# Identity times identity on TensorE inside the normalization helper of a four-layer decoder kernel

## The chip, the cores and the metric

The kernel runs on one NeuronCore of one Trainium2 chip. The metric is the device time of one execution in microseconds, given as the median of several runs. Beside these runs stands one execution that the hardware profiler recorded. All rows below come from that one.

## The reference, cut to what matters

The model takes 4 sequences of 512 tokens, 128 wide, and a context of 77 tokens for each sequence. It adds twelve sublayers to the residual x, three in each of four layers: a self attention, an attention over the context, and a feed-forward sublayer (mixtures of experts, or, in the third layer, an attention with mixed experts and a dense network behind it). Each sublayer reads a normalized x:

```
def _layernorm(x, axis=-1, eps=1e-05):
    m = jnp.mean(x, axis=axis, keepdims=True)
    v = jnp.var(x, axis=axis, keepdims=True)
    return (x - m) / jnp.sqrt(v + eps)
...
x = x + _L1_attn_ref(_layernorm(x, axis=-1), L1_attn_wq, L1_attn_wk, L1_attn_wv, L1_attn_wo, L1_attn_bo)
x = x + _L1_xattn_ref(_layernorm(x, axis=-1), ctx_1024, L1_xattn_w_sim, L1_xattn_b_sim, L1_xattn_W_qv, L1_xattn_b_qv)
x = x + _L1_ffn_ref(_layernorm(x, axis=-1), ...)
```

With the normalization inside the third layer's feed-forward sublayer that is followed by a projection, the kernel's helper is called 13 times. All matrix products are of float32 or of its split halves.

## The kernel before

The tokens lie on 128 partitions in 16 tiles of 128 tokens by 128 features: four batches of four tiles. The residual `T.X`, the normalized tokens `T.LNX` and their transpose `T.LNT` stay in SBUF for the whole kernel. Sublayers run one after another. Each is first a call of `layernorm` (L100), a block of its own, and then one block or more of work. At a block's end every engine waits for all others.

Inside the block of `layernorm`, SyncE issues the next stage's loads. VectorE computes the statistics that the sublayer before has not left (most have left all), adds epsilon to the variances (L132), ScalarE takes the root (L168), and VectorE makes the reciprocal and the shift (L136, L137). Then both scale tiles of 128x128: VectorE the even ones (L142), ScalarE the odd ones (L171). TensorE waits for the four tiles of a batch and transposes them into PSUM bank c (L162; banks 2 and 3 are called `twin`). ScalarE copies banks 0 and 2 to `T.LNT` (L176), VectorE banks 1 and 3 (L149), each after its last scaled tile. Batch 3's copy on VectorE is the last thing of the block, or nearly.

`T.ident` is the identity of 128x128 in float32, loaded once before the first stage. PSUM bank 7 isn't used by `layernorm`.

One call, that of the third layer's context attention (stage `l2x`, L1919), passes `aside`: work of that stage that needs no normalized tokens. Its part on TensorE is three products of 308 columns (L1899, L1900), issued ahead of the transposes. On VectorE two multiplications that read them (L1906) and four additions (L1911) stand between the scaled tiles and the copies.

What follows a normalization, where it matters below: `l1a` (L1461, L1463), `l1m` (the router, L1079, 32 products of 64 columns, then the shared expert, L1028 and L1029), `l0m` (the same with 16 columns), `l2a` (L1737), and `l2f` (L3029).

Of the kernel before, what the change touches and what calls it, by code (L numbers as in the profile page):

```python
# [21 lines left out]
P = 128  # L22
# [27 lines left out]
def chain(T, dve):  # L50

    def link(ins):
        T.dve_steps += 1
        ins.then_inc(T.dve_step, 1)
        dve.wait_ge(T.dve_step, T.dve_steps)
    return link


def token_stats(nc, T, link, src, tiles):

    for t in tiles:
        out = nc.vector.bn_stats(T.ln_stats[:, t, :], src[:, t, :])
    link(out)
    for t in tiles:
        out = nc.vector.bn_aggr(T.ln_mv[:, t, :], T.ln_stats[:, t, :])
    T.ln_known += tiles
    return out
# [32 lines left out]
def layernorm(nc, T, src, dst, dstT, loads=(), load_sem=None, more=(), more_sem=None, begun=(), times=None, aside=None, columns=None, eps=1e-5, zeros=()):  # L100

    n = T.ln_calls
    T.ln_calls += 1
    with nc.Block() as block:
        @block.sync
        def _(sp):
            for to, frm in loads:
                sp.dma_start(to, frm).then_inc(load_sem, 16)  # L110
            for to, frm in more:
                sp.dma_start(to, frm).then_inc(more_sem, 16)
            for to, frm, here in begun:
                sp.dma_start(to, frm).then_inc(here, 16)

        @block.gpsimd
        def _(pool):
            for sems, _ in T.used:
                for s in sems:
                    pool.sem_clear(s)  # L120
            for buffer in zeros:
                nc.gpsimd.memset(buffer, 0.0)

        @block.vector
        def _(dve):
            link = chain(T, dve)
            unknown = [t for t in range(NT) if t not in T.ln_known]
            if unknown:
                link(token_stats(nc, T, link, src, unknown))
            T.ln_known = []  # L130
            if times is None:
                nc.vector.tensor_scalar(T.ln_var_eps[:, :], T.ln_mv[:, :, 1], eps, None, ALU.add).then_inc(T.ln_var, 1)  # L132
            else:
                nc.vector.tensor_scalar(T.ln_var_eps[:, :], T.ln_mv[:, :, 1], times, eps, ALU.mult, ALU.add).then_inc(T.ln_var, 1)
            dve.wait_ge(T.ln_std, n + 1)
            link(nc.vector.reciprocal(T.ln_rstd[:, :], T.ln_var_eps[:, :]))  # L136
            nc.vector.scalar_tensor_tensor(T.ln_shift[:, :], T.ln_mv[:, :, 0], -1.0, T.ln_rstd[:, :], ALU.mult, ALU.mult)\  # L137
                .then_inc(T.ln_scaled, 1)
            dve.wait_ge(T.ln_scaled, n + 1)
            for t in range(NT):  # L140
                if t % 2 == 0:
                    nc.vector.tensor_scalar(dst[:, t, :], src[:, t, :], T.ln_rstd[:, t:t + 1], T.ln_shift[:, t:t + 1],  # L142
                                            ALU.mult, ALU.add).then_inc(T.ln_even, 1)
            if aside is not None:
                aside[1](dve)
            for c in range(1, B, 2):
                dve.wait_ge(T.ln_turned, B * n + c + 1)
                if columns is None:
                    nc.vector.tensor_copy(dstT[:, c * S:(c + 1) * S], T.bank[c][:, :])  # L149
                else:  # L150
                    nc.vector.tensor_scalar(dstT[:, c * S:(c + 1) * S], T.bank[c][:, :], columns[:, 0:1], columns[:, 1:2],
                                            ALU.mult, ALU.add)

        @block.tensor
        def _(pe):
            if aside is not None:
                aside[0](pe)
            for c in range(B):
                pe.wait_ge(T.ln_even, NT // 2 * n + TPB // 2 * (c + 1))
                pe.wait_ge(T.ln_odd, NT // 2 * n + TPB // 2 * (c + 1))  # L160
                for t in range(TPB):
                    last = nc.tensor.transpose(T.bank[c][:, t * P:(t + 1) * P], dst[:, c * TPB + t, :], T.ident[:, :])  # L162
                last.then_inc(T.ln_turned, 1)

        @block.scalar
        def _(act):
            act.wait_ge(T.ln_var, n + 1)
            nc.scalar.activation(T.ln_var_eps[:, :], T.ln_var_eps[:, :], ACT.Sqrt).then_inc(T.ln_std, 1)  # L168
            act.wait_ge(T.ln_scaled, n + 1)
            for t in range(1, NT, 2):  # L170
                nc.scalar.activation(dst[:, t, :], src[:, t, :], ACT.Identity, bias=T.ln_shift[:, t:t + 1],  # L171
                                     scale=T.ln_rstd[:, t:t + 1]).then_inc(T.ln_odd, 1)
            for c in range(0, B, 2):
                act.wait_ge(T.ln_turned, B * n + c + 1)
                if columns is None:
                    nc.scalar.activation(dstT[:, c * S:(c + 1) * S], T.bank[c][:, :], ACT.Copy)  # L176
                else:
                    nc.scalar.activation(dstT[:, c * S:(c + 1) * S], T.bank[c][:, :], ACT.Identity, bias=columns[:, 1:2],
                                         scale=columns[:, 0:1])
            if aside is not None:  # L180
                aside[2](act)
    for _, held in T.used:
        held.close()
    T.used = []
# [3160 lines left out]
```

## Time and profile before

| | |
|---|---|
| median of three runs | 2374.95 us |
| the three runs | 2374.86, 2374.95, 2377.97 us |
| the profiled execution | 2371.28 us |
| its span | 2369.5 us |
| TensorE busy in it | 2107.8 us, 89% |
| VectorE busy | 1673.9 us, 71% |
| ScalarE busy | 1216.1 us, 51% |
| GpSimd busy | 1148.7 us, 48% |
| granted TensorE clock, mean | 0.94 of full |

A busy TensorE isn't TensorE at its peak: matmuls are pipelined, and a row's duration holds the latency too, so that what a product costs in a stream is the distance between starts. The granted clock is the share of full speed that the chip gave TensorE: 1.00 stands for 2.4 GHz, 0.50 for 1.2 GHz. In the first 31.9 us the profile has no record of it and shows 1.00 throughout.

### The profile page before, as it was taken

What the parts mean: (1) busy time and instruction counts of PE and PEld (TensorE: products, weight loads), DVE (VectorE), ACT (ScalarE), POOL (GpSimd) and SP (SyncE); (2) the same over time, 40 slices, a digit from 0 to 9 for tenths busy, and PEclk for the clock granted to TensorE, in tenths of its full rate; (3) what the DMA queues carried; (4) which work ended last, traced back from release to release, by engine and by line L of the source; (5) the groups of instructions that cost most, each with busy time, mean ns of one, the idle gap of its engine ahead of it and who ended that gap; (6) DMA issues with size and microseconds to landing.
All of it is one profiled execution on the core that took longest, in us unless ns stands there. A gap on an engine that the chain in (4) does not pass through costs nothing. (4 is left out here: it accounts for less than half of the span.)

```text
span 2369.5 us, 37661 instructions
## 1 busy us (share of the span) xinstructions
PE 2107.8 (89%) x12788; PEld 1466.2 (62%) x12788; DVE 1673.9 (71%) x3561; ACT 1216.1 (51%) x2586; POOL 1148.7 (48%) x1343
## 2 busy tenths in 40 slices
PE   6999789667899997759999999999999986979889
PEld 3666557556588875545666666666666644647666
DVE  5778777654788884667777777777766665379578
ACT  6888645322466654535445454444444443444455
POOL 5332027101499981137676766667665623004255
PEclk8999979866999998979999999999999997989899
DMA  1000006000566630022343333343443341000085
GB/s 50 2 2 2 7 21 155 8 6 22 125 153 157 155 83 24 1 70 59 96 101 76 99 84 95 79 108 79 92 92 78 73 89 43 8 1 1 14 201 125
DMA packets 65048, 161.92 MB, mean 68 GB/s; under 512 B 8139, under 2 KB 19147, under 8 KB 57560
## 3 DMA queue, kind: packets, MB, share of 16 engines
q1 hardware_dynamic: 64856, 159.50, 28.9%
q8 instruction: 103, 1.69, 0.3%
q14 instruction: 89, 0.73, 0.1%
HBM read 156.46 MB, written 3.01 MB: 67 GB/s over the span
## 5 line engine op out<-in xcount | busy, mean ns | idle before, releaser
L2636 PE MATMUL bank<-l2h_og,l2h_wo 128*128 128x512 f32 x512 | 260.4, 593 | 1.6 <-DVE LNT L2897 1.6
L2746 ACT ACTIVATE l2h_pr<-twin,l2h_nmx 128x512 f32<-128x512 f32 x256 | 176.0, 688 | 150.5 <-PE bank L2625 104.9
L2738 ACT ACTIVATE l2h_prT<-bank 128x512 f32<-128x512 f32 x256 | 151.9, 593 | 194.6 <-PE bank L2625 194.6
L1215 POOL TENSOR_TENSOR l1m_hid_lo<-l1m_hid,l1m_hid_hi 128x512 fp32r<-128x512 f32 x128 | 210.3, 1663 | 46.0 <-ACT l1m_hid_hi L1142 45.6
L2900 DVE TENSOR_REDUCE l2h_nmx<-twin 128x2 f32<-128x1024 f32 x128 | 156.1, 1220 | 90.7 <-PE twin L2614 90.6
L2975 POOL TENSOR_TENSOR l2h_vs<-l2h_vg 128x256 f32<-128x256 f32 x256 | 192.9, 754 | 19.9 <-DVE l2h_vg L2873 19.9
L2873 DVE TENSOR_TENSOR l2h_vg<-bank,l2h_gv 128x512 f32<-128x512 f32 x256 | 174.9, 683 | 34.2 <-POOL l2h_vs L2975 20.9
L2885 DVE TENSOR_TENSOR l2h_og<-bank,l2h_gt 128x512 f32<-128x512 f32 x256 | 173.1, 680 | 3.8 <-PE bank L2636 2.7
L2970 POOL TENSOR_TENSOR l2h_plain<-l2h_plain,l2h_rotated 128x512 f32<-128x512 f32 x64 | 82.6, 1291 | 169.5 <-DVE l2h_rotated L2866 169.5
L2625 PE MATMUL bank<-ident,l2h_pr 128*128 128x128 f32 x1024 | 160.8, 279 | 0.0
L2625 PEld LDWEIGHTS bank<-ident,l2h_pr 128*128 128x128 f32 x1024 | 116.7, 140 | 66.9 <-issue 43.4
L2599 PE MATMUL bank<-l2h_w_hi,l2h_x_hi 128*128 128x512 f32 x256 | 150.8, 589 | 4.1 <-DVE l2h_vg L2873 3.9
L405 ACT ACTIVATE l0a_pr<-l0a_sc,l0a_nmx 128x128 f32<-128x128 f32 (+3 forms) x256 | 133.3, 553 | 22.2 <-DVE l0a_nmx L290 21.4
L1265 DVE TENSOR_TENSOR l1m_hid<-l1m_prod,l1m_c 128x512 f32<-128x512 f32 x128 | 135.6, 1059 | 4.4
L2978 POOL TENSOR_TENSOR l2h_vs<-l2h_vs 128x128 f32<-128x128 f32 x256 | 121.5, 475 | 20.1
L2650 PE MATMUL bank<-l2h_prT,l2h_v 128*64 128x256 f32 x1024 | 124.7, 385 | 0.0
L1257 DVE TENSOR_TENSOR l1m_prod<-bank,l1m_gate 128x512 f32<-128x512 f32 x128 | 88.1, 688 | 45.7 <-ACT l1m_gate L1177 33.8
L1177 ACT ACTIVATE l1m_gate<-bank 128x512 f32<-128x512 f32 x128 | 76.6, 599 | 84.6 <-PE bank L1020 84.6
L2356 POOL TENSOR_TENSOR l3x_pr<-l3x_pr,l3x_rs 128x1232 f32<-128x1232 f32 x16 | 35.9, 2249 | 171.6 <-DVE l3x_rs L2378 171.6
L2983 POOL TENSOR_TENSOR l2h_v<-l2h_vs 128x64 f32<-128x64 f32 x256 | 82.2, 321 | 74.9 <-PE bank L2650 57.2
L2650 PEld LDWEIGHTS bank<-l2h_prT,l2h_v 128*64 128x64 f32 x1024 | 68.2, 136 | 75.2 <-issue 41.7
L2636 PEld LDWEIGHTS bank<-l2h_og,l2h_wo 128*128 128x128 f32 x512 | 95.5, 189 | 28.5 <-issue 3.8
(625 smaller groups left out, 5823.3 us busy)
## 6 DMA issues: line engine op xcount, KB each, us to landing
l2h_gt<-l2m_gate_rows SPq DMA_DIRECT2D x128, 512.0 KB, 7.3
l1m_c<-l1m_weights SPq DMA_DIRECT2D x62, 512.0 KB, 6.5
l3m_c<-l3m_weights SPq DMA_DIRECT2D x30, 512.0 KB, 6.6
l0m_c<-l0m_weights SPq DMA_DIRECT2D x14, 512.0 KB, 6.8
l1m_w<-in_l1m_pairs SPq DMA_DIRECT2D x32, 192.0 KB, 6.5
l2h_fresh<-in_l2m_wqkv SPq DMA_DIRECT2D x8, 768.0 KB, 4.2
l2h_wo<-in_l2m_wo SPq DMA_DIRECT2D x8, 512.0 KB, 3.9
l0m_w<-in_l0m_pairs SPq DMA_DIRECT2D x8, 192.0 KB, 5.3
```

The source lines that it names most:

```text
L1215: nc.gpsimd.tensor_tensor(hid_lo[:, h % RING, :], hid[:, h % HELD, :], hid_hi[:, h % RING, :], ALU.subtract)\
L1265: nc.vector.tensor_tensor(hid[:, h % HELD, :], p, cslot[s][:, blk * S:(blk + 1) * S], ALU.mult).then_inc(hidden, 1)
L2599: out = nc.tensor.matmul(pj[at % 2][:, :], x[:, b * S + t * P:b * S + (t + 1) * P], w[:, QK + h * S:QK + (h + 1) * S], start=(p == 0), sto ...
L2625: out = nc.tensor.transpose(tbank[:, c * P:(c + 1) * P], pr[:, h, c * P:(c + 1) * P], T.ident[:, :])
L2636: nc.tensor.matmul(ybank[:, :], wo[s][:, e, :], og[:, e % 4, :], start=(e == 0), stop=(e == E - 1))\
L2650: out = nc.tensor.matmul(obank[g % 2][h * HD:(h + 1) * HD, half * 2 * P:(half + 1) * 2 * P], v[:, g % 2, h * TPB + c, :], prT[:, half, h, ...
L2738: nc.scalar.activation(prT[:, j // 2 % 2, h, :, j % 2 * P:(j % 2 + 1) * P], tbank[:, :].rearrange("p (c q) -> p c q", c=TPB), ACT.Copy).th ...
L2746: nc.scalar.activation(pr[:, h, :], sbank[:, h, :], ACT.Exp, bias=nmx[:, k % 2, h:h + 1], accum_out=rs[:, g % 2, t, h:h + 1]).then_inc(exp ...
L2873: nc.vector.tensor_tensor(vg[:, u % 2, :, :], pj[at % 2][:, :].rearrange("p (e d) -> p e d", e=E), spread(gv_h[s][:, b * TPB + t, h, :], H ...
L2885: nc.vector.tensor_tensor(og[:, e % 4, :], obank[g % 2][:, :], gt[:, e // 4, e % 4, :], ALU.mult)\
L2900: nc.vector.tensor_reduce(nmx[:, k % 2, :], sbank[:, :, :], axis=AX, op=ALU.max, negate=True)\
L2975: nc.gpsimd.tensor_tensor(vs[:, u % 2, :, :], vg[:, u % 2, 0:4, :], vg[:, u % 2, 4:8, :], ALU.add)\
```

## The change

Two groups of matrix products are added to TensorE's part of `layernorm`. Each multiplies the identity by itself and writes 128 columns of bank 7, which nothing reads there. Nine stand at the block's start, ahead of `aside`'s products, and two ahead of each batch but the first, before the wait for its scaled tiles. Nothing is removed or moved. In 13 calls that makes 195 products.

```
         @block.tensor
         def _(pe):
+            def keep_busy(times):
+
+                for _ in range(times):
+                    nc.tensor.matmul(T.bank[7][:, 0:P], T.ident[:, :], T.ident[:, :], start=True, stop=True)
+            keep_busy(9)
             if aside is not None:
                 aside[0](pe)
             for c in range(B):
+                if c:
+                    keep_busy(2)
                 pe.wait_ge(T.ln_even, NT // 2 * n + TPB // 2 * (c + 1))
                 pe.wait_ge(T.ln_odd, NT // 2 * n + TPB // 2 * (c + 1))
                 for t in range(TPB):
```

## Rows read from the trace of the kernel before

**Rows 1.** The page: busy time (share of the span), and granted clock in 40 slices.
```profile
PE 2107.8 (89%) x12788; PEld 1466.2 (62%) x12788; DVE 1673.9 (71%) x3561; ACT 1216.1 (51%) x2586; POOL 1148.7 (48%) x1343
...
PEclk8999979866999998979999999999999997989899
```

**Rows 2.** Timeline of the fourth normalization, ahead of stage l1a: start, duration, instructions, idle before.
```profile
434.81 0.17 DVE L132 TENSOR_SCALAR ln_var_eps<-ln_mv 128x16 f32<-128x16 f32 x1 [0.30 <-PEq L969]
...
435.76 3.19 ACT L171 ACTIVATE LNX<-X,ln_shift,ln_rstd 128x128 f32<-128x128 f32 x8 [0.53 <-DVE ln_shift L137]
...
436.78 1.94 PE L162 MATMUL bank<-ident,LNX 128*128 128x128 f32 x8 [6.44 <-ACT LNX L171]
438.52 1.92 PE L162 MATMUL twin<-ident,LNX 128*128 128x128 f32 x8
...
440.47 0.69 DVE L149 COPY LNT<-twin 128x512 f32<-128x512 f32 x1 [1.01 <-PE twin L162]
...
441.46 2.04 PE L1461 MATMUL bank<-LNT,l1a_wq 128*128 128x512 f32 x2 [1.03 <-PEq L106]
```

**Rows 3.** Line 162 in all 13 normalizations: durations min/median/max in ns.
```profile
L162 PE MATMUL bank<-ident,LNX x104: 272/421/448, 14.1 to 2222.0; 128*128 128x128 f32 x104
```

**Rows 4.** Timeline, streams of 128-column products at each level of the clock.
```profile
563.77 0.64 PE L1632 MATMUL bank<-l1c_w,l1c_hq 128*128 128x128 f32 x2
...
564.20 0.63 PE L1633 MATMUL bank<-l1c_w,l1c_ehq 128*128 128x128 f32 x2
...
946.62 3.65 PEld L1771 LDWEIGHTS bank<-l2a_v,l2a_e 128*128 128x128 f32 x32 [1.78 <-DVE l2a_v L1829]
```

**Rows 5.** Windows: length, busy (count) by engine, PEclk, DMA share, GB/s; runs of TensorE at 1.2 GHz.
```profile
441.40:444.90 3.50, 3.44 (x6) 2.15 (x7) 0.92 (x1) 0.00 (x0) 0.00 (x0) 0.50 0.01 2
444.90:446.00 1.10, 1.10 (x5) 0.59 (x4) 0.00 (x0) 0.00 (x0) 0.00 (x0) 0.99 0.00 0
500.00:502.90 2.90, 2.88 (x14) 2.84 (x15) 1.83 (x6) 2.72 (x8) 0.00 (x0) 0.50 0.22 74
502.90:503.50 0.60, 0.48 (x4) 0.24 (x2) 0.09 (x1) 0.55 (x1) 0.00 (x0) 0.96 0.00 0
...
561.00:567.70 6.70, 6.25 (x29) 6.16 (x30) 0.36 (x1) 1.35 (x2) 0.00 (x0) 0.50 0.00 0
567.90:568.50 0.60, 0.41 (x4) 0.22 (x2) 0.15 (x1) 0.00 (x0) 0.00 (x0) 1.00 0.00 0
```

**Rows 6.** Timeline of the eighth normalization, the one with `aside`.
```profile
952.81 1.72 PE L1899 MATMUL bank<-l2p_ctxT,l2p_wk 128*128 128x308 f32 x4 [2.35 <-PEq L1729]
...
955.83 0.86 DVE L1906 TENSOR_TENSOR l2p_krot<-bank,l2p_ktrig_kept 128x308 f32<-128x308 f32 x2
...
959.27 0.68 DVE L149 COPY LNT<-twin 128x512 f32<-128x512 f32 x1
```

**Rows 7.** Windows behind normalizations 6 (l1m), 7 (l2a) and 10 (l2f).
```profile
577.30:588.20 10.90, 10.88 (x37) 8.66 (x38) 2.52 (x4) 6.51 (x10) 5.96 (x5) 0.50 0.01 2
...
897.70:902.20 4.50, 4.42 (x9) 2.38 (x10) 0.85 (x2) 0.00 (x0) 1.66 (x3) 0.50 0.09 33
1960.30:1963.80 3.50, 3.48 (x4) 1.50 (x5) 1.40 (x1) 0.69 (x1) 3.20 (x3) 0.50 0.01 2
```

**Rows 8.** Timeline, the first transposes of normalizations 3 and 12, with the idle time before.
```profile
324.54 1.94 PE L162 MATMUL bank<-ident,LNX 128*128 128x128 f32 x8 [3.49 <-ACT LNX L171]
...
2116.71 1.86 PE L162 MATMUL bank<-ident,LNX 128*128 128x128 f32 x8 [4.63 <-ACT LNX L171]
```

**Rows 9.** Windows: the 16-column router behind normalization 3, what follows it, and normalization 12.
```profile
329.20:332.20 3.00, 2.98 (x27) 3.00 (x28) 0.00 (x0) 2.98 (x6) 2.30 (x2) 1.00 0.00 0
332.40:339.00 6.60, 6.60 (x12) 3.35 (x13) 4.68 (x15) 2.96 (x4) 3.60 (x4) 0.50 0.00 1
...
2116.70:2117.40 0.70, 0.63 (x4) 0.39 (x4) 0.70 (x4) 0.70 (x3) 0.00 (x0) 1.00 0.00 0
2117.50:2120.80 3.30, 2.77 (x12) 2.31 (x12) 1.51 (x4) 2.45 (x6) 0.00 (x0) 0.50 0.00 0
```

More of the change, by code:

```diff
@@ L155, in _, with keep_busy @@
         def _(pe):
+            def keep_busy(times):
+                for _ in range(times):
+                    nc.tensor.matmul(T.bank[7][:, 0:P], T.ident[:, :], T.ident[:, :], start=True, stop=True)
+            keep_busy(9)
             if aside is not None:
@@ L158, in _ @@
             for c in range(B):
+                if c:
+                    keep_busy(2)
                 pe.wait_ge(T.ln_even, NT // 2 * n + TPB // 2 * (c + 1))
```

## Prediction

> **What bounds the kernel now.** I read the page first. TensorE is busy for 89% of the span, but its clock isn't at full speed everywhere: the row of slices has sixes, sevens and eights, and several lie where normalizations are [rows 1]. So two questions follow: what bounds a normalization, and at which clock TensorE runs in it and right behind it.
>
> The timeline of one normalization answers the first [rows 2]. From VectorE's first instruction (434.81) a chain of small ones leads to the scaled tiles (435.76), and TensorE's first transpose starts at 436.78, 1.97 us after entry. TensorE is idle through all of these 1.97 us, and for some time before them too: 6.44 us in all here, 3.49 to 4.63 in seven others [rows 2, 8]. Then 16 transposes run until VectorE's copy of the last bank begins at 440.47, and TensorE's next stage starts at 441.46 after 1.03 idle. ScalarE scales its last tile until 438.95, so the last batch would be ready about 1.5 us before that copy: it is TensorE that ends the block, because it is slow. The two groups of eight transposes start 1.74 apart, 0.217 each. The source view says that this is the usual case: the median transpose lasts 421 ns, the fastest 272 [rows 3].
>
> The second I read from windows around each call. Of 13 normalizations none ran at 2.4 GHz throughout, seven ran at 1.2 GHz from the first transpose to the last, three (5, 11 and 13) rose in the last few transposes, 8 halfway, and 9 and 12 began high and fell after a batch. Behind four of them (4, 6, 7, 10) the next stage starts low and TensorE's busy time fills the stretch: 3.5, 11.0, 4.5 and 3.5 us [rows 5, 7].
>
> **The price of one added product.** The trace has no product of the identity with itself, but it has streams of the same shape. At 1.2 GHz pairs of 128-column products start 0.43 apart, 0.215 each; at 2.4 GHz 32 weight loads of the same shape take 3.65, 0.114 each, with the matmuls hidden behind them [rows 4]. The bounds are therefore 0.107 (half of the low price) and 0.215.
>
> **The nine at the start.** At the low clock 9 x 0.215 = 1.94 us against 1.97 of waiting: they just fit. At the high clock they take about 1 us and leave 1 us of idleness. The cover is the chain of variance, root, reciprocal, shift and two tiles on each of the other engines. It is gone if the first product starts late: the first pair of a low stream above takes 0.59 instead of 0.43, so up to 0.15 can stick out. I take 0.1 in each of 12 calls: **+1.2 us**, between 0 and 1.8. The first call has much more cover, since it computes its statistics inside the block.
>
> **The six between the batches.** At the low clock they are not covered. A batch costs 4 x 0.217 = 0.87, while ScalarE gives the next one every 0.80 (3.19 for eight tiles). The queue is TensorE's own, so all six are added: 6 x 0.215 = 1.29 us at the block's end, if the clock stays low. The transposes behind them are late, then the copies of banks 2 and 3, then the block's end. At the high clock a batch with its two takes 0.65 and fits into 0.80, the last batch ends 0.43 after ScalarE's last tile, and the last copy begins at about 439.6 instead of 440.47: 0.85 earlier.
>
> So all hangs on where the clock rises. What the added products change is that TensorE works without a break from entry, 1.94 us earlier, until the end: up to 6.7 us instead of 3.6. The trace shows when unbroken runs at the low clock brought a rise: after 2.9 us (500.02 to 502.9, fourteen transposes, with 4.3 idle ahead), after 3.5 us (441.4 to 444.9), and only after 6.1 where the run began at 561.7 [rows 5]; no unbroken run of wide products lasted longer without one. I take the rise as equally likely anywhere from 2.7 to 6.1 us after entry, 0.7 to 4.1 after the first transpose. If it comes x after the first transpose, of 3.45 + 1.29 = 4.74 of low-clock work the rest is halved: the end is at 2.37 + x/2, not before 2.87 (ScalarE). The mean is 3.6, against 3.45 where it was low throughout and a mean of 3.35 over the twelve. That is +0.25 each, 12 x 0.25 = **+3.0 us**, with bounds of -0.85 and +1.3 each.
>
> Here a rule of the Trainium skill speaks against the change, so it is weighed. In the window from 500.0 to 502.9 TensorE did only float32 transposes, and at its end the clock was up, for two further normalizations as well [rows 5]. The page "TensorE: Matmul & The Clock Gate", section "Part 4: PE-mode transpose", says that transposes don't count as busy for the clock. By that rule the sixteen transposes would help nothing, the added products alone would seldom bring a rise, and the sum of this paragraph and the last would be about +17 us instead of +4; the trace disagrees with it.
>
> **The eighth normalization.** There nine products stand ahead of three of the stage's own that are already on the path: VectorE goes straight from its scaled tiles to L1906 at 955.83, with no idle time before it, and L1906 reads two of them; four additions and the copies behind it, to 959.95, end the block [rows 6]. Nothing covers the nine. They cost 0.97 to 1.94, by the clock, and I take the middle: **+1.5 us**.
>
> **What follows.** Behind 4, 7 and 10 the next stage's first 3.5, 4.5 and 3.5 us ran at 1.2 GHz with TensorE busy all the time [rows 5, 7]. At 2.4 GHz they take half: -1.75, -2.25 and -1.75. The idle gap between the block and the next is 1.03 us [rows 2], and ahead of normalization 12 the high clock outlived 4.63 us of idleness by a batch [rows 8, 9]. So if it rose in the normalization I expect it to last in 85 of 100: **-4.9 us**. Behind 6 stand 32 router products of 64 columns and the shared expert's, 11.0 us at the low clock, TensorE the one everybody waits for [rows 7]. Halved that is -5.5. But narrow products don't hold the clock well: behind 3 the 16-column router began at the high clock and lost it at 332.3 without a pause [rows 9]. With 64 columns I give it 60 of 100: **-3.3 us**. The same stretch behind 3 was lucky, since the clock was up for nearly all of its router (27 of 32 in 3.0 us, 0.11 each [rows 9]). On average it will have half of that: **+1.4 us**. Behind 2, 5 and 9 TensorE idles again before it has much work, so nothing is carried over; behind 11 and 12 the clock was high already.
>
> **Sum.** 1.2 + 3.0 + 1.5 - 4.9 - 3.3 + 1.4 = -1.1 us. On the profiled execution's 2371.28 that is 2370.2; on the median of the runs, 3.7 us above it, 2373.8. The unchanged kernel's own runs lie 3.1 us apart, and I put that down, as a guess, to the clock rising and falling at other places in each. What a measurement can tell from no change is about 0.2%, 4.7 us.
>
> **The rivals.**
>
> *The clock stays up.* TensorE idles only 1.5 to 2.7 us before entry in most calls, once the 1.97 behind it are filled. If the clock never falls there, or rises as early as it can, each of twelve normalizations gives about 0.6 (of at most 0.85), the stages behind give 11.3, and with 8 and the start's cost the sum is -7.2 - 11.3 + 1.0 + 0.5 = -17: 2358. For it: normalization 12 had the high clock for its first batch after 4.6 us of idling and lost it only 0.7 us later [rows 8, 9]. Against it: in 4, 7, 10 and 11 TensorE idles 4.5 us and more before entry even so, and at the high clock the nine leave 1 us idle again. Half of this effect, -8, is more likely than all of it: 2367.
>
> *The rise is given back.* The clock rises in the normalizations, but the block's gap or the next stage's narrow products lose it, and nothing is gained behind: 1.2 + 3.0 + 1.5 + 1.4 = +7: 2382. It decides the sign as soon as less than about 7 us comes from behind.
>
> *The clock doesn't rise in time.* If it falls within the nine, they are done early at the high clock, an idle piece follows, and the next rise comes only after the block. Then the six cost their full 1.29: 12 x 1.29 + 1.8 + 1.9 = +19: 2394, and if this holds for half of the calls, 2383. The deciding point is a rise later than about 2.2 us after the first transpose. For it: seven normalizations now have no rise in 3.6 us of dense work. Against it: the work is now nearly twice as long.
>
> *Nothing happens*, because every added product is hidden. At the low clock the six can't be, so this I count with the forecast.
>
> **How the numbers follow.** The forecast, gains and costs within 4.7 us of each other, gets 0.48; the clock that stays up, in part or in full, 0.30; the rise given back 0.12; the rise too late 0.10. Of the second a little ends inside the bound and of the forecast a little outside, which evens out: faster 0.30, same 0.48, slower 0.22. The likeliest case alone spans 2370 to 2379. The range must reach into both neighbours: 2363 (a bit more than half of the first rival) to 2382 (the second).
>
> **What would show it.** In the profile after, L162 should follow the nine without a gap at the low clock, its first start 1.97 to 2.1 after L132. Windows should show the clock at 1.00 before the last batch in most normalizations, and VectorE's last copy 5.1 to 7.0 after L132 (5.66 now). Line 1461, L1737 and L3029 should start at 1.00. L1906 should start 1 to 2 us later after L134 than now. The prediction is wrong if windows stay at 0.50 through the block, if the last copies move beyond 6.5 as a rule, or if the stages behind start low as before.

## The result and the profile after

The change made the kernel slower: 0.7% where it was first timed, 1.0068 times the kernel before (95% interval 1.0048 to 1.0088; median 2396.11 us against 2375.65, six runs each), and 1.0037 (1.0018 to 1.0055) in a second set (median 2386.09 us of nine against 2380.01). Its times lie in two groups, to which the fourth experiment returns, and the median goes with how many fall in each. The forecast was no change, 2373.8 us within 2363 to 2382. The profiled execution took 2398.32 us with a span of 2396.5, 27.0 more than the span before. Its line for the added products on the page, in the columns of part 5 (busy, mean ns of one, idle before):

```profile
L159 PE MATMUL bank<-ident 128*128 128x128 f32 x390 | 72.5, 347 | 54.1 <-PEq L3086 16.6
```

The source adds 195 products and the trace counts 390. Lines below L153 have moved by seven, so that L162, L171 and L176 are now L169, L178 and L183. The timeline of normalization 4, to set beside [rows 2]:

```profile
442.60 4.18 PE L159 MATMUL bank<-ident 128*128 128x128 f32 x18 [4.46 <-PEq L976]
...
443.56 3.19 ACT L178 ACTIVATE LNX<-X,ln_shift,ln_rstd 128x128 f32<-128x128 f32 x8 [0.53 <-DVE ln_shift L137]
...
446.57 1.06 PE L169 MATMUL bank<-ident,LNX 128*128 128x128 f32 x4
447.43 0.85 PE L159 MATMUL bank<-ident 128*128 128x128 f32 x4
...
448.99 0.60 PE L169 MATMUL twin<-ident,LNX 128*128 128x128 f32 x4
449.43 0.61 PE L159 MATMUL bank<-ident 128*128 128x128 f32 x4
...
449.88 0.60 PE L169 MATMUL twin<-ident,LNX 128*128 128x128 f32 x4
450.51 0.69 DVE L149 COPY LNT<-twin 128x512 f32<-128x512 f32 x1 [1.08 <-PE twin L169]
```

Read it against [rows 2] step by step. Nine products are eighteen records and fill TensorE for 3.97 us, from 442.60 to 446.57, where the tiles were ready at 1.97. Two products are four records. At the high clock a group of four transposes starts 0.45 after the four records ahead of it, and the next pair of products 0.44 after the transposes: a batch now takes 0.89, where ScalarE gives one every 0.80 and where, with the tiles all ready, transposes alone would take 0.44. L132 starts at 442.61, so that the last copy starts 7.90 after it; before, it was 5.66.

The windows (columns as in [rows 5]) show that the clock did what the added work was to bring, in the normalizations and right behind them:

```profile
446.50:451.10 4.60, 3.98 (x30) 3.74 (x28) 1.28 (x2) 1.45 (x3) 0.00 (x0) 0.85 0.02 4
451.50:454.00 2.50, 2.49 (x10) 1.79 (x10) 0.92 (x1) 0.00 (x0) 0.00 (x0) 1.00 0.01 3
...
904.40:908.70 4.30, 4.24 (x20) 4.27 (x21) 2.74 (x11) 3.41 (x9) 1.15 (x1) 0.50 0.58 150
908.80:911.50 2.70, 2.70 (x27) 2.70 (x26) 0.69 (x1) 1.12 (x2) 0.00 (x0) 1.00 0.82 246
912.80:917.00 4.20, 2.97 (x13) 1.85 (x14) 0.90 (x3) 1.24 (x4) 1.63 (x3) 1.00 0.00 0
```

The stretch behind normalization 4, low for 3.5 us in [rows 5], is now at 1.00, and so is the one behind 7, low for 4.5 in [rows 7].

To see where 27.0 us went I cut both traces at each start of L132 (L134 in normalization 8) and at the end of the last copy to `T.LNT`. The first piece is the normalization from there on, the second what lies between it and the next one's L132.

| piece | before, us | after, us | difference |
|---|---|---|---|
| 13 normalizations, sum | 82.3 | 101.5 | +19.2 |
| normalization 4 | 6.35 | 8.59 | +2.2 |
| normalization 8 | 7.14 | 9.27 | +2.1 |
| normalization 9 (after: clock high throughout, as in 13) | 6.27 | 6.06 | -0.2 |
| behind 4, 7 and 10 | 56.88, 55.33, 46.93 | 55.08, 53.15, 45.18 | -5.7 |
| behind 6 | 314.12 | 316.30 | +2.2 |
| behind 9 | 931.46 | 938.04 | +6.6 |
| behind 13, to the end | 145.0 | 147.7 | +2.7 |
| behind 1, 2, 3, 5, 8, 11 and 12 | | | +2.1 |

The normalizations are the greater part. Of the rest, the stage behind 9 is the largest. A window of each trace, from the same stage:

```profile
1062.80:1093.10 30.30, 24.74 (x139) 15.84 (x139) 17.73 (x24) 15.88 (x33) 23.09 (x40) 1.00 0.38 78
```

```profile
1076.00:1093.10 17.10, 13.95 (x42) 7.95 (x41) 5.76 (x8) 5.08 (x9) 9.97 (x21) 0.60 0.11 26
```

The first is of the kernel before, the second of the one after, where the stage begins 13 us later; both start 40.7 to 40.9 us into it. Before, the clock was up for good by then; after, it was down for most of the stretch (0.60 granted). No instruction there differs.

### The profile page after: what moved, and what is told of

The parts are those of the page before. It is cut to its first block and busy times, and to the rows that moved or that the text cites. A ratio compares the mean times of both kernels' runs of the same rounds, so it can differ in the third digit from the quotient of the medians.

```text
span 2396.5 us, 38441 instructions
## 1 busy us (share of the span) xinstructions
PE 2154.4 (90%) x13178; PEld 1515.9 (63%) x13178; DVE 1678.4 (70%) x3561; ACT 1217.2 (51%) x2586; POOL 1149.5 (48%) x1343
## 3 DMA queue, kind: packets, MB, share of 16 engines
q8 instruction: 106, 1.74, 0.3%
## 5 line engine op out<-in xcount | busy, mean ns | idle before, releaser
L159 PE MATMUL bank<-ident 128*128 128x128 f32 x390 | 72.5, 347 | 54.1 <-PEq L3086 16.6
L1184 ACT ACTIVATE l1m_gate<-bank 128x512 f32<-128x512 f32 x128 | 76.6, 599 | 84.8 <-PE bank L1027 84.8
```

## The experiments

All edits are to the changed kernel. From the fifth experiment on the pairs between the batches are out, even where the lines shown don't say it; only the eighth has one product there. Ratios are to the kernel before, timed on the same chip in the same rounds.

**The same products as transposes.** Each float32 product becomes one transpose, which is one record.

```
-                    nc.tensor.matmul(T.bank[7][:, 0:P], T.ident[:, :], T.ident[:, :], start=True, stop=True)
+                    nc.tensor.transpose(T.bank[7][:, 0:P], T.ident[:, :], T.ident[:, :])
```

> All 195 added products become transposes of the identity into the same bank (one pass over 128 columns each, where a float32 product is two: the profile after counts 18 matmul records for nine). Theory A, the price of a product was off by two and the rest of the working stands: added work halves, 9 x 0.215 = 1.94 us fits into the 1.97 us of waiting, so the first transpose of the real work is at 1.97 to 2.1 us after L132, the sum over the 13 normalizations (82.3 us before, 101.5 after) comes to 82 to 87, and the median is 2370 to 2378. Theory B, the price of a product is not the matter and any added work on TensorE in this place costs (a disturbance of the stages behind, a later clock): 2385 or more, and the stages behind normalization 9 stay 6 us longer than before. Theory C, transposes don't lift the clock: normalizations near 88 us in sum and the stages behind 4, 7 and 10 as long as before, 2378 to 2384.

Measured: 0.9992 (0.9979 to 1.0004), median 2377.59 us, no difference. The normalizations last 84.8 us in sum, and the first real transpose comes 1.97 us after L132 in twelve of the thirteen. This is theory A's outcome, and B falls by the time. One sign that B named did appear: the stage behind 9 took 940.35 us, 8.9 more than before. So that stage grows without the price of a product, and its 6.6 us in the table aren't part of that price. C falls too: the normalizations are not near 88, and behind 4, 7 and 10 the stages take 55.1, 51.45 and 45.2 us. What I had forecast for the change is what this kernel does.

**Only the nine at the start.**

```
-                if c:
-                    keep_busy(2)
```

> Only the nine products at the start. Theory A: TensorE reaches the first real transpose 3.4 to 4.0 us after L132 where the clock is low at entry, as with the change, so some 15 of the 19 us that the normalizations became longer stay, the six between batches give back 0.3 to 0.5 each: normalizations 94 to 97 us in sum, the median 2384 to 2392. Theory D, the six between the batches are what costs: the sum near 86 and the median under 2380.

Measured: 0.9966 (0.9954 to 0.9978), median 2373.86 against 2380.01 for the kernel before: faster. The normalizations last 83.2 us, not the 94 to 97 that I expected: theory A was wrong about where in the change the cost sits, and D was right. The timeline of its normalization 4 shows why:

```profile
434.46 3.61 PE L159 MATMUL bank<-ident 128*128 128x128 f32 x18 [4.46 <-PEq L974]
434.46 0.17 DVE L132 TENSOR_SCALAR ln_var_eps<-ln_mv 128x16 f32<-128x16 f32 x1 [0.30 <-PEq L974]
437.90 1.04 PE L167 MATMUL bank<-ident,LNX 128*128 128x128 f32 x8
438.77 1.04 PE L167 MATMUL twin<-ident,LNX 128*128 128x128 f32 x8
...
439.85 0.69 DVE L149 COPY LNT<-twin 128x512 f32<-128x512 f32 x1 [0.18 <-PE twin L167]
```

The nine do delay the first transpose, to 3.44 us after L132. But by then nearly all scaled tiles lie ready, and the clock has risen, so eight transposes take 0.87 instead of 1.74 [rows 2]. The last copy starts 5.39 after L132, sooner than the 5.66 of before. The clock in the second group of transposes and just ahead of it:

```profile
438.00:439.80 1.80, 1.80 (x17) 1.57 (x15) 0.69 (x1) 1.52 (x4) 0.00 (x0) 1.00 0.01 2
```

**Only the two between batches.** `keep_busy(9)` is taken out.

> Only the two products ahead of batches 1 to 3. Theory A: the first real transpose is at 1.97 us as before; six products are 2.6 us at the low clock and 1.3 at the high one, part of it in ScalarE's shadow: normalizations +0.7 to +1.3 each, 91 to 98 in sum, less 3 us behind normalizations that now end at the high clock; median 2379 to 2388. Theory D: as slow as the whole change, 2390 or more.

Measured: 1.0055 (1.0043 to 1.0067), median 2393.4: D's case, as slow as the whole change. The normalizations last 106.8 us, above A's 91 to 98 and 5.3 more than with the whole change: put in ahead of these pairs, the nine gave time back. In number 4, TensorE reaches its first transposes at 1.97 us as before and then alternates:

```profile
442.63 1.08 PE L168 MATMUL bank<-ident,LNX 128*128 128x128 f32 x4 [6.44 <-ACT LNX L177]
443.51 1.06 PE L159 MATMUL bank<-ident 128*128 128x128 f32 x4
444.37 1.06 PE L168 MATMUL bank<-ident,LNX 128*128 128x128 f32 x4
```

A pair of products costs 0.86 us at the low clock, as much as the four transposes that wait behind it; three pairs are 2.6 us.

**The change once more.**

> The change as it is, once more, on the same chip. Its six times so far fall in two groups, 2383 to 2386 and 2396 to 2398. Theory A says only that the mean is about 2394 and that the gap between the groups lies in which stages run at 1.2 GHz, so a profile of another execution differs in the stages behind the normalizations, not in the normalizations by more than 3 us. Theory B: the slow group is a fixed cost, the times gather at 2396 and 10 us of it sit in the same stage, the one behind normalization 9.

Measured: 1.0037 (1.0018 to 1.0055), times from 2382.5 to 2398.8 with a gap between 2386.1 and 2392.6. The profile is again of the slower group: 101.1 us of normalizations and 938.04 behind 9. So it doesn't tell the groups apart. Two further profiles were taken for that.

> The change unchanged, for a profile of its faster group (2382 to 2386), which about half of its 15 times so far belong to; both profiles so far are of the slower one (2396.5 and 2397.0 us of span). If this one is of the faster group: by the clock's theory the 13 normalizations last 98 to 102 us as in the others and the 10 to 14 us lie in several stages, the one behind normalization 9 (938.0 us in both) at 931 to 935 among them. By the rival, that the added products themselves are costlier in the slower group, the normalizations last 90 us or less.

> The same once more, with the same expectations, since a single profile falls into the faster group only about every second time.

Both fell in the slower group as well (2398.29 and 2399.84 us). Their normalizations last 102.7 and 101.9 us. In the first the stage behind 9 took 933.94, four less than in the others, and the whole was no faster. None of the four profiles is of the faster group, so no trace shows in which stages the two part. The granted clock of the 17 executions does tell them apart: its mean over the span is 0.947 to 0.951 in the seven up to 2386.5 us, and 0.942 to 0.946 in the ten from 2392.6. The means of the groups, 0.9491 and 0.9438, are apart by some 25 us more at the low clock; if TensorE sets the pace in them, half of that is lost, 12 to 13 us (an estimate), and the groups' mean times lie 12.3 apart. That the clock makes the gap is thus likely; what decides between the two cases stays open.

**The nine, but not in normalization 8.**

```
-            keep_busy(9)
+            if aside is None:
+                keep_busy(9)
```

> The nine products at the start alone, and none in normalization 8, where three products of the stage wait behind them. With the nine, normalization 8 lasted 8.71 us against 7.14 before. Theory E, the nine are paid back everywhere but there: normalization 8 back at 7.1, the rest as with the nine alone, 1 to 2 us faster than those, 0.995 to 0.997 of the kernel before. Rival F, the nine gain by the clock in the stage behind normalization 8 too: 54.3 us there becomes 55.9 again and the time is that of the nine alone.

Measured: 0.9978 (0.9964 to 0.9992), no faster than with it (0.9966). Normalization 8 is back at 7.13, but the stage behind it at 55.88: rival F's numbers. The nine cost 1.58 us there, and the clock that they lift gives 1.57 back in the projection behind.

**Nine transposes at the start, nothing between.** The edits of the first two experiments together.

> Nine transposes of the identity at the start, one pass each, and nothing between the batches. Theory G, what pays is the time TensorE works without a break ahead of the real transposes: 1.94 us instead of 3.9, so the clock rises in fewer normalizations before their transposes; the first real transpose is at 1.97, normalizations 5.6 to 6.4 each, 77 to 80 in sum (83.2 with nine products), the stages behind 4, 7 and 10 partly at the low clock; 2372 to 2377 where the kernel before is at 2380. Rival H, added transposes don't count for the clock: normalizations as before, 82 in sum, and the time of the kernel before.

Measured: 0.9963 (0.9950 to 0.9976), median 2369.68 against 2377.48; normalizations 76.8 us in sum, behind 4, 7 and 10 54.4, 51.46 and 45.18. Theory G holds for the normalizations, but not in that the rise comes in fewer of them: in ten they take 5.64 to 5.92 us, against 5.95 to 6.47 before. The first and the last take 6.36 and 6.25, the eighth 7.13.

```profile
435.90 2.15 PE L159 MATMUL bank<-ident 128*128 128x128 f32 x9 [4.47 <-PEq L974]
...
437.88 1.48 PE L167 MATMUL bank<-ident,LNX 128*128 128x128 f32 x8
439.42 1.40 PE L167 MATMUL twin<-ident,LNX 128*128 128x128 f32 x8
```

```profile
435.90:437.80 1.90, 1.90 (x9) 1.75 (x9) 1.55 (x7) 1.16 (x4) 0.00 (x0) 0.50 0.30 83
437.90:440.70 2.80, 2.60 (x17) 2.00 (x16) 1.79 (x6) 2.80 (x8) 0.00 (x0) 0.85 0.28 79
```

Nine records fit into the 1.97 us, the clock rises among the real transposes, and ScalarE's last tile ends the block. TensorE did nothing but transposes here, and rival H falls. The Trainium skill's page "TensorE: Matmul & The Clock Gate", section "Part 4: PE-mode transpose", has it that transposes don't count as busy; for these float32 ones the trace disagrees.

**Six products behind the last batch, with the nine.**

```
                 last.then_inc(T.ln_turned, 1)
+            keep_busy(6)
```

> Nine products at the start, and six more behind the last batch's transposes, where they run beside the copies and nobody waits. Theory I, the six cost only because they stand ahead of batches: the normalizations stay at the 83 us of the nine alone, the time within 3 us of the nine alone, or below it where the clock now outlives the gap to the next block (behind 6 above all, 317 us there with the nine alone against 314). Rival J, added work on TensorE is what costs wherever it stands: near the change's own 2386 to 2396. At 1.2 GHz six products are 2.6 us against some 1.8 us until the next block, so up to 0.8 can stick out in a normalization where the clock hasn't risen.

Measured: 1.0019 (1.0008 to 1.0030), median 2383.72 against 2377.48. Theory I fell: behind the last batch the six cost too. Rival J, that they cost wherever they stand, comes nearer, though the time is below J's 2386 to 2396. The trace shows a place that neither named, the block's end:

```profile
442.69 1.50 PE L159 MATMUL bank<-ident 128*128 128x128 f32 x12
444.49 1.10 PE L1467 MATMUL bank<-LNT,l1a_wq 128*128 128x512 f32 x2 [0.30 <-PEq L106]
```

The next block waits for TensorE, which is done at 444.19, while VectorE's copy ended at 443.58. The next stage starts 0.91 after that copy's end; with the nine alone it starts 0.30 after it (440.54, 440.84). That is 0.6 in this call. Over the thirteen, this gap sums to 16.4 us, with the nine alone to 10.1: 6.3 more, beside +3.2 in the normalizations (86.4). The two make up 9.5 of the 14.8 us by which this profile's span exceeds that of the nine alone; the rest lies in the stages behind.

**One product between the batches.** `keep_busy(1)` for `keep_busy(2)`.

> The change with one product between the batches instead of two. Theory A' (each product ahead of a batch is two passes, 0.215 us at the high clock and 0.43 at the low one, and none of it is hidden once the nine have let the tiles be ready): half of the step from the nine alone (83 us in the normalizations, 0.9966) to the change (101 us, 1.0037 to 1.0068): normalizations 90 to 94, the time 0.999 to 1.002 of the kernel before. Rival K, one product of 0.215 at the high clock fits behind a batch of 0.43 into ScalarE's 0.80 a batch: normalizations as with the nine alone.

Measured: 1.0015 (1.0000 to 1.0030); normalizations 90.7 us. Both lie where A' put them, and K falls: the sums run 83.2, 90.7, 101.5 for none, one and two.

**Eighteen transposes for nine products.** The edits of the sixth experiment, with `keep_busy(18)`.

> Eighteen transposes at the start, nothing between the batches: as many passes over 128 columns as nine products. Theory A'' (only passes count, for time and clock alike): the profile looks like that of the nine products alone, first real transpose 3.3 to 4.0 us after L132 in most normalizations, normalizations 82 to 84 in sum, the time 0.995 to 0.998 of the kernel before. Rival L, a product costs or lifts the clock otherwise than two transposes: outside these.

Measured: 0.9975 (0.9963 to 0.9987), normalizations 85.9 us, first real transpose 3.2 to 3.9 us after L132 in most. The time is that of nine products within the intervals. The sum is 1.9 us above the 82 to 84 that I had set as the border to rival L, so by its letter L isn't ruled out. A product counts as two transposes to within that: the sums are 83.2 and 85.9, and what the 2.7 between them are due to wasn't tried.

**Nine transposes, and four behind the last batch.**

> Nine transposes at the start as in the kernel of that name (76.8 us of normalizations, 0.9963), and four more transposes behind the last batch. They take 0.43 us at the high clock and 0.86 at the low one, and the engines reach the next block some 1.2 us or more behind TensorE's last transpose, so they are hidden: normalizations 76 to 78. Theory M, they keep the clock up over the gap: stages behind 4, 6, 7 and 10 at 54.4, 314 to 315, 51.5 and 45.2 or less, the time 0.993 to 0.996. Rival N, they change nothing that counts: 0.995 to 0.998.

Measured: 0.9974 (0.9958 to 0.9990), normalizations 78.1 us: N's case. The gap behind the copy stays at 0.30 us in most calls, and nothing is gained.

## Why the prediction was wrong

**The step that failed is "The price of one added product".** It read 0.215 us at the low clock off "pairs of 128-column products" and "32 weight loads of the same shape" [rows 4]. Those rows count records, and a float32 product of the source is two of them: x18 for nine in the trace after. The pair that I called two products is one. The price is 0.43 at the low clock and 0.22 at the high one (a pair of products in 0.86 and in 0.44), twice the bounds that I gave. The same kernel made of one-record operations (the first experiment) came out as no change, at 2377.6.

**The nine at the start** were to fit, 1.94 against 1.97, for +1.2 us. They took 3.4 to 4.0 where the clock was low, so my term was wrong by some 1.5 to 2 us a call. Yet it cost nothing in the end: alone, they left the normalizations at 83.2 us (82.3 before), since the transposes behind them ran from ready tiles at the high clock, and made the kernel faster. I had no term for that payback.

**The six between the batches** carry the loss. I had 1.29 us for them if the clock stays low, and "fits into 0.80" at the high clock. At the true price a batch with its pair takes 0.89 against 0.80 at the high clock, and 1.72 at the low one. Behind the nine, moreover, 0.80 isn't the limit: the tiles are ready, and each record of the six adds in full. 12 records at 0.11 are 1.3 a call even at the high clock, 17 in thirteen calls; removing them took the normalizations from 101.5 to 83.2. My term of +3.0 held the six and the gain from the clock together. It can't be measured by itself, but my three terms inside the normalizations were +5.7 in sum and measured +19.2, of which the six are 18.3.

**The rise of the clock** came as forecast. At the last batch it was up in all thirteen normalizations, none of which had it throughout before. It came 3.0 to 6.2 us after entry in the eleven that had a low stretch, where I had 2.7 to 6.1. There is some luck in the upper end: the run "from 561.7" that I took it from wasn't unbroken, since TensorE idled 0.45 us ahead of 563.18. One of my signs of being wrong did appear, last copies beyond 6.5 us after L132 as a rule: they start at 6.6 to 8.6 in eleven of thirteen. They are late by the price of the products, with the clock up.

**Normalization 8** was right as a mechanism: nothing covers the nine. Sized +1.5, it measured +2.1, of which 1.6 belong to the nine (8.71 with them alone).

**What follows.** Behind 4, 7 and 10 I had -1.75, -2.25 and -1.75 before the factor for chance and measured -1.80, -2.18 and -1.75. Behind 6 I had -3.3 and got +2.2: 316.30 against 314.12, and 314.6 to 318.0 in the experiments, although the clock was up in its first 9.9 us and the 32 router products took 3.3 us less. The first row is of the kernel before, the others are of the one after:

```profile
592.00 1.10 PE L1035 MATMUL bank<-l1m_hid,l1m_shared 128*128 128x512 f32 x2 [2.13 <-DVE l1m_hid L1236]
...
602.21 2.05 PE L1042 MATMUL bank<-l1m_hid,l1m_shared 128*128 128x512 f32 x2 [6.50 <-DVE l1m_hid L1243]
...
589.50:598.00 8.50, 6.21 (x33) 3.95 (x32) 4.41 (x3) 6.81 (x11) 6.63 (x6) 1.00 0.00 1
598.10:608.30 10.20, 6.09 (x7) 2.52 (x8) 7.82 (x61) 0.59 (x2) 0.00 (x0) 0.50 0.00 1
```

"TensorE the one everybody waits for" was wrong from there on. Behind the router VectorE works through a chain of its own before it gives TensorE the next tile (L1236, now L1243). It began this chain 3.2 us earlier than before but came to that tile only 0.95 us earlier, as two of its instructions lasted 2.66 and 1.51 us instead of 1.23 and 0.68; why they did was not tried. TensorE idled 6.50 us instead of 2.13, its clock fell at 598.1, and the next six pairs of records took 8.27 us to start where they had taken 5.23. Gained 0.95, lost 3.04: that is the +2.1 that the rest of the stage carries along. Behind 3, +1.4 forecast, -1.4 measured.

**The rivals.** The slower ones got 0.22 together. The one that gave the right time, 2394, did so by a clock that doesn't rise. Had I counted on it, the number would have been luck: the trace shows that the clock rose and the products cost double.

**What stays open.** Some 13 us of this one profile lie in stages that the change doesn't touch: the 2.2 behind 6, and 11 in stages for most of which I had put nothing. The 6.6 behind normalization 9 can be followed product by product. The first product is 1.8 us late, as TensorE waits longer for a load (3.61 us instead of 1.78):

```profile
1038.04 3.44 PE L2702 MATMUL bank<-l2h_wsel,LNT 128*128 128x256 f32 x8 [3.61 <-DMA l2h_wsel<-in_l2m_wsel]
```

SyncE issued that load 4.43 us after L132, not 2.71; why is not shown. Some 4 us into the stage the products are 3.5 us late, 52 us into it 6.5, and from there to its end the distance hardly changes. In the stage's first 60 us the clock is low for 37.5 us, against 23.9 before. So there the loss is a later load and then a lower clock. For the other stages the clock is likely and was only argued. They vary from kernel to kernel without a difference in code: 931.4 to 940.4 us behind 9, 265.0 to 268.3 behind 1. The kernel before, too, ran between 2364.7 and 2384.7 us over all sets, with a mean granted clock from 0.944 in the fastest execution to 0.935 in the slowest, and its profile of 2371.28 is one of the quicker ones.

## What to carry to other kernels

Count the records of a known source line before pricing from a row: here a float32 product is two records on TensorE and a transpose one, and the factor of two decided the sign. Work that keeps an engine awake is free only while nothing of its own queue is ready behind it: nine transposes in 1.97 us of real waiting gave 0.37%, and the same kind of work ahead of ready batches, or running on past the last copy into the block's end, took more than that back. An instruction that delays the first item of a batch isn't lost if the last item sets the end and runs faster for it. And before a faster stretch is booked as a gain, ask what the engine waits for behind it: behind 6 TensorE was 3.3 us faster, waited 4.4 us longer and lost its clock in that wait.

## What the runs showed of the hardware that was not expected

A float32 transpose of 128x128 is one record on TensorE (0.217 us from start to start at 1.2 GHz, 0.109 at 2.4), a float32 product of the same shape two such records. Float32 transposes raised the granted clock as well as products did: it was up before the last transpose in twelve of the thirteen normalizations both with nine products and with eighteen transposes in front, and its mean over the span was 0.944 to 0.951 and 0.945 to 0.950 in their runs. A clock that had risen was lost again in one wait of TensorE of 6.50 us, 2.4 us after its last product had ended. And one and the same program's times lay in two groups 6 us or more apart (up to 2386.5, and from 2392.6), with a single core at work; the executions of the slower group had the lower granted clock, without exception.
